# The end of one round's convolutions among the next round's: a hand-written order without a loop

## What is computed

```python
CONVS = [(128, 10, 5)] + [(128, 3, 2)] * 4 + [(128, 2, 2)] * 2     # channels, taps, stride
h = x[:, None, :]
for w, g, b, s in zip(conv_ws, ln_gs, ln_bs, strides):
    h = _conv1d(h, w, s)
    h = jnp.swapaxes(h, -2, -1)
    h = _fp32_layernorm(h, g, b)
    h = jnp.swapaxes(h, -2, -1)
    h = jax.nn.gelu(h, approximate=False)
```

## Time and profile before

| | us |
|---|---|
| median of 3 runs | 964.54 |
| lowest, highest | 959.35, 964.63 |
| the profiled execution, whole | 964.83 |
| its span, first to last instruction | 963.1 |
| TensorE busy in the span | 762.8 |
| VectorE busy | 612.2 |
| ScalarE busy | 306.3 |
| GpSimd busy | 214.3 |
| mean granted TensorE clock | 0.896 |

### The profile page before, as it was taken

How to read it: one execution, slowest core, us unless ns; L and a number is a source line. 1 busy time by engine, 2 the same in 40 slices (tenths; PEclk the granted TensorE clock), 3 DMA queues, 4 the chain that set the end, 5 groups by cost and what they waited for, 6 DMA issues and landing times. The chain is left out here.

```text
span 963.1 us, 11862 instructions
## 1 busy us (share of the span) xinstructions
PE 762.8 (79%) x4033; PEld 560.7 (58%) x4033; DVE 612.2 (64%) x1445; ACT 306.3 (32%) x505; POOL 214.3 (22%) x253
## 2 busy tenths in 40 slices
PE   0069998899989998999998625728888886489987
PEld 0026665565546664565555424617788885389977
DVE  4918555784658555244645545899888889744377
ACT  0043334333532434333312120202232331236433
POOL 3000000000000000000000030653678778318401
PEclk9999998899979898899997556859899999889999
DMA  1350420016000320000000070000000000200000
GB/s 56 43 124 1 75 65 1 0 23 118 0 2 0 68 60 0 1 1 0 1 1 1 0 303 0 1 0 1 1 0 0 0 0 0 74 1 1 1 1 25
DMA packets 22554, 25.31 MB, mean 26 GB/s; under 512 B 17052, under 2 KB 21212, under 8 KB 21404
## 3 DMA queue, kind: packets, MB, share of 16 engines
q1 hardware_dynamic: 22508, 24.74, 10.7%
HBM read 21.05 MB, written 3.66 MB: 26 GB/s over the span
## 5 line engine op out<-in xcount | busy, mean ns | idle before, releaser
L565 PE MATMUL ps<-h,w 128*128 128x400 f32 x720 | 294.8, 554 | 1.1 <-ACT h L633 0.9
L565 PEld LDWEIGHTS ps<-h,w 128*128 128x128 f32 x720 | 141.4, 203 | 106.9 <-issue 104.4
L725 DVE COPY h<-ps 128x800 f32<-128x800 f32 (+2 forms) x58 | 56.6, 975 | 97.8 <-PE ps L565 97.1
L578 PEld LDWEIGHTS ps<-averager,sq 128*100 128x100 f32 (+2 forms) x1024 | 101.9, 175 | 22.3 <-ACT sq L626 18.5
L578 PE MATMUL ps<-averager,sq 128*100 128x1 f32 (+2 forms) x1024 | 102.4, 230 | 7.8 <-ACT sq L626 7.3
L626 ACT ACTIVATE sq<-h 128x800 f32<-128x800 f32 (+2 forms) x58 | 49.9, 860 | 179.1 <-DVE h L725 179.1
L1062 PE MATMUL pt<-for_pe,ident 128*128 128x156 f32 (+2 forms) x420 | 76.9, 348 | 35.3 <-DVE for_pe L1256 35.3
L1062 PEld LDWEIGHTS pt<-for_pe,ident 128*128 128x128 f32 x420 | 69.0, 219 | 42.6 <-DVE for_pe L1256 38.7
L633 ACT ACTIVATE h<-h,lnp 128x800 f32<-128x800 f32 (+2 forms) x58 | 60.6, 1045 | 84.6 <-DVE h L756 82.8
L756 DVE TENSOR_TENSOR h<-h,ps 128x400 f32<-128x400 f32 (+2 forms) x116 | 60.0, 559 | 39.3 <-PE ps L594 39.3
L605 ACT ACTIVATE h<-ps,lnp 128x800 f32<-128x800 f32 x64 | 63.4, 1011 | 64.1 <-PE ps L526 63.9
(11 more groups left out here) (269 smaller groups left out, 1131.7 us busy)
## 6 DMA issues: line engine op xcount, KB each, us to landing
late<-windows_dram SPq DMA_DIRECT2D x24, 375.0 KB, 7.5
gate_w<-in_gate_w SPq DMA_DIRECT2D x1, 3456.0 KB, 13.0
up_w<-in_up_w SPq DMA_DIRECT2D x1, 3456.0 KB, 19.3
windows_dram<-parts SPq DMA_DIRECT2D x12, 250.0 KB, 4.9
acts<-in_down_w SPq DMA_DIRECT2D x1, 1728.0 KB, 8.2
w<-in_w SPq DMA_DIRECT2D x1, 1024.0 KB, 5.7
xs<-in_x SPq DMA_DIRECT2D x4, 252.5 KB, 4.4
out_tokens<-hidden SPq DMA_DIRECT2D x6, 96.0 KB, 1.6
```

The source lines that it names most:

```text
L565: mm = pe.matmul(out, w[:, L.first_tap + t, :], source(l, s, 2 * p + c, t), start=(t == 0), stop=(t == L.taps - 1))
L578: mm = pe.matmul(var_ps[0:L.w, at:at + 1], sq[:, n["var"] % 2, c, q * L.w:(q + 1) * L.w], averager[:, 0:1], start=True, stop=True)
L725: nc.vector.tensor_copy(joined(l, s, p, r).rearrange("p (c b) t -> p c b t", c=2), ypair[n["bank"]][:, :, 0:L.cols].rearrange("p c (b t) - ...
```

## The change

`round_plan`, walked once per round, becomes `tower_plan`, one list for all four rounds, and the loops are gone on all engines. Three things are moved in the order:

- What followed `conv(2,1,1)` in the first three rounds, that is `var` and `norm` of (2,1), its `rows` and `scale`, and all of layer three, now stands among the first four to five steps of layer one of the next round (`past` in the diff).
- Signals 0 to 8 of the next round were spread over layers two and three. They now stand all in layer two: 0 in `conv(2,1,0)`, 1 and 2 behind it, 3 in `conv(2,1,1)`, 4 behind it, then 5 to 8 in a row.
- The preparation for the round after next begins in layer two: parts 0 to 10 stand around the four steps of layer two, part 11 at the start of the next round, 12 and 13 before the fourth and fifth step of layer one. The first round's own parts 0 to 10 stand before its first step.

So that steps of two rounds can be in flight together, `rparts` and `rows` get four sets in place of two, `norm` waits for a set to be free, the variances of each layer get PSUM columns of their own, every `var` waits for the read of the `norm` before it, and `rows` waits for the copy of the `rows` before it.

```diff
+        if r == 0:
+            prep(1, 0, PREP_LATE)
+        prep(r + 1, PREP_LATE, PREP_LATE + 1)
+        conv(1, 0, 0, first(9), before(var(2, 1, 1, past), norm(2, 1, past)))
+        if past >= 0:
+            conv(3, 0, 0, first(10), var(1, 0, 0), of=past)
+            conv(1, 0, 1, before(rows(2, 1, past), var(3, 0, 0, past), scale(2, 1, 0, 1, of=past)))
+        else:
+            conv(1, 0, 1, first(10), var(1, 0, 0))
+        before(scale(2, 1, 2, 3, of=past), norm(3, 0, past))()
+        conv(1, 0, 2, first(11), var(1, 0, 1))
+        if past >= 0:
+            conv(3, 1, 0, rows(3, 0, past), var(1, 0, 2), of=past)
+        prep(r + 1, PREP_LATE + 1, PREP_LATE + 2)
+        conv(1, 0, 3, first(12), *([] if past >= 0 else [var(1, 0, 2)]), before(var(3, 1, 0, past), scale(3, 0, 0, 1, of=past), norm(3, 1, past)))
+        prep(r + 1, PREP_LATE + 2, PREP_LATE + 3)
+        conv(1, 1, 0, first(13), var(1, 0, 3), norm(1, 0))
+        before(rows(3, 1, past), scale(3, 1, 0, 1, of=past))()
+        conv(1, 1, 1, first(14), rows(1, 0), var(1, 1, 0), scale(1, 0, 0, 1))
+        scale(1, 0, 2, 3)()
+        conv(1, 1, 2, first(15), var(1, 1, 1), scale(1, 0, 4, 5))
+        scale(1, 0, 6, 7)()
+        conv(1, 1, 3, var(1, 1, 2))
+        prep(r + 2, 0, 2)
+        conv(2, 0, 0, var(1, 1, 3), norm(1, 1))
+        conv(2, 0, 1, rows(1, 1), var(2, 0, 0), scale(1, 1, 0, 1))
+        scale(1, 1, 2, 3)()
+        prep(r + 2, 2, 4)
+        conv(2, 1, 0, ahead(0), scale(1, 1, 4, 5), var(2, 0, 1), norm(2, 0))
+        ahead(1)()
+        scale(1, 1, 6, 7)()
+        prep(r + 2, 4, 6)
+        ahead(2)()
+        conv(2, 1, 1, ahead(3), rows(2, 0), var(2, 1, 0), scale(2, 0, 0, 1))
+        prep(r + 2, 6, 8)
+        ahead(4)()
+        scale(2, 0, 2, 3)()
+        prep(r + 2, 8, PREP_LATE)
+        ahead(5, 6, 7, 8)()
+        if not last:
+            return
...
-        rparts = sb("rparts", [100, 2, 4, 96], BF16)
-        rows = sb("rows", [96, 2, 400], BF16)
+        rparts = sb("rparts", [100, SETS, 4, 96], BF16)
+        rows = sb("rows", [96, SETS, 400], BF16)
...
+                    elif what == "var":
+
+                        pe.wait_ge(y_taken, number_of(plan, "conv", r, l, s, p, "pair") + 1)
+                        if n["norm"]:
+                            pe.wait_ge(var_read, n["norm"])
...
+                        if n["rows"]:
+                            pe.wait_ge(rows_ready, n["rows"])
...
+                        if n["norm"] >= SETS:
+                            dve.wait_ge(rstd_turned, n["norm"] - SETS + 1)
```

More of the change, by code:

```diff
@@ L73 @@
 TAPS = 16
+SETS = 4
+PREP_LATE = K0 + 1
 FILLERS = 10
@@ L118, in newton_rsqrt, with tower_plan @@
     steps.settle()
-def round_plan(last):
+def tower_plan():
     order = []
[L129 to L230, removed]
@@ L231, in round_plan @@
+    for r in range(ROUNDS):
+        of_round(r)
     return counted(order)
@@ L237, in counted @@
     n = dict.fromkeys(("pair", "half", "conv", "var", "norm", "rows", "scale", "gelu", "first", "prep"), 0)
-    out, bank, held = [], 0, None
-    users = [("first", -2), ("first", -1)]
-    for what, l, s, p in order:
+    n["pair"] = AHEAD
+    out, bank, held = [], AHEAD % 2, None
+    users = [("first", AHEAD - 2 + (AHEAD % 2)), ("first", AHEAD - 1 - (AHEAD % 2))]
+    for what, r, l, s, p in order:
         step = dict(n)
@@ L253, in counted, with number_of, gelus_before @@
             step["bank"], held = held, None
-        out.append((what, l, s, p, step))
+        out.append((what, r, l, s, p, step))
         n[what] += 1
         n["pair"] += what in ("conv", "first")
[L257 to L277, removed]
+    convs = [x[1:5] for x in out if x[0] == "conv"]
+    assert convs == [x[1:5] for x in out if x[0] == "var"]
+    return out
+def number_of(plan, what, r, layer, slot, p, kind):
+    return next(n[kind] for *key, n in plan if key == [what, r, layer, slot, p])
+def gelus_before(plan, r, layer, slot):
+    return {p: n["gelu"] for what, of, l, s, p, n in plan if (what, of, l, s) == ("gelu", r, layer, slot)}
 def conv_tower(nc, io, res, top):
-    body, per = round_plan(False)
-    last, _ = round_plan(True)
+    plan = tower_plan()
     sem = lambda n: top.enter_context(nc.semaphore(n))
@@ L363, in chunk @@
             if l == 3:
-                return h3[:, bass.ds(r, 1), slot, a:a + n, 0:L.pos].rearrange("p o b t -> p (o b) t")
+                return h3[:, r, slot, a:a + n, 0:L.pos]
             if l == 4:
@@ L382, in source, with batch_taken @@
             return (h4, h5)[l - 5][:, a:a + n, cut]
[L384 to L391, removed]
-                return batch + 1
[L393 to L399, removed]
+        def batch_taken(r, batch):
+            if r == 0 and batch < AHEAD:
+                return batch + 1
+            return number_of(plan, "first", r, 0, batch // GROUP, batch % GROUP, "pair") + 1
+        set_of = {(r, l, s): n["norm"] % SETS for what, r, l, s, p, n in plan if what == "norm"}
+        var_at = lambda l, k: 32 * l + k
         def joined(l, s, p, r):
@@ L409, in joined @@
             if l == 3:
-                return h3[:, bass.ds(r, 1), s, a:a + n, 0:L.pos].rearrange("p o b t -> p (o b) t")
+                return h3[:, r, s, a:a + n, 0:L.pos]
             if l == 4:
@@ L458, in _ @@
                 attention_weights(sp, io, res)
[L460 to L472, removed]
+                for r in range(1, ROUNDS):
+                    scratch = windows(r, r < ROUNDS - 1)
+                    for slot, batch in enumerate((GROUP - 1, ROUND - 1)):
+                        sp.wait_ge(y_ready, batch_taken(r - 1, batch))
+                        back(scratch, slot)
             @block.gpsimd
@@ L504, in _ @@
                                        base=-32 * a, pattern=[[-1, 8], [0, P]], channel_multiplier=1).then_inc(s_const, 1)
-                with pool.Fori(1, ROUNDS) as r:
+                for r in range(1, ROUNDS):
                     spread_phases(r)
@@ L535, in _ @@
                         pe.wait_ge(y_taken, b - 1)
[L536 removed]
+                    first(b, b % 2)
                 pe.wait_ge(weights_ready, 2)
[L539 to L550, removed]
[L551 to L595 removed]
@@ L636, in _ @@
-                for_rounds(act, run)
+                    first(b // GROUP, b % GROUP, b % 2, b)
+                for what, r, l, s, p, n in plan:
+                    L = LAYERS.get(l)
+                    if what == "first":
+                        first(s, p, n["bank"], n["pair"])
+                    elif what == "conv":
+                        act.wait_ge(y_copied, n["conv"] + 1)
+                        if n["conv"] >= 2:
+                            act.wait_ge(var_done, n["conv"] - 1)
+                        act.activation(sq[:, n["conv"] % 2, :, 0:L.cols].rearrange("p c (b t) -> p c b t", t=L.pos),
+                                       joined(l, s, p, r).rearrange("p (c b) t -> p c b t", c=2), ACT.Square).then_inc(y_taken, 1)
+                    elif what == "gelu":
+                        act.wait_ge(scaled, n["scale"])
+                        both = joined(l, s, p, r)
+                        act.activation(both, both, ACT.Gelu, scale=lnp[:, 2 * l:2 * l + 1],
+                                       bias=lnp[:, 2 * l + 1:2 * l + 2]).then_inc(gelu_done, 1)
```

262 lines of the change are left out of this document (146 added, 116 removed).

## The result

| | before | changed |
|---|---|---|
| median us | 962.63 (6 runs) | 978.24 (6 runs) |
| lowest, highest | 959.35, 966.20 | 977.12, 982.69 |
| profiled execution | 964.83 | 982.69 |
| its span | 963.1 | 981.0 |

The changed kernel takes 1.0175 times the time of the kernel before (95% interval 1.0151 to 1.0199). It is slower by 15.6 us. Its profiled execution is the slowest of its six, 4.5 us above their median, where that of the kernel before lies 2.2 us above its own; so two sets of rows laid side by side show 17.9 us (981.0 - 963.1), some 2 more than the medians. 979.8 us was forecast.

A forecast was written before the change was run, and what follows sets the result against it. TensorE was taken as the bound, losing time where it waits or runs at the lower clock. 963.1 us plus 3.0 (-39.5 + 16.8 + 15.4 + 10.3) plus 12 for clock, with 1.7 around the span, gave 979.8; range 959 to 992.

The forecast's parts named there:

- The end of a round: Behind `conv(2,1,1)`, TensorE waits for ScalarE's queue: 5.9 us lost in two rounds, 5.0 in the third, 16.8 in all.
- the sign to look for: Right behind `conv(2,1,1)`, four `first`s about 1 us apart, TensorE waiting for ScalarE, 5 to 6 us in all.
- Layer two: Waits for VectorE's late copy of `conv(2,1,0)` and for ScalarE: 6.1 us in two rounds, 3.2 in the third, 15.4 in all.
- Layer one: VectorE's queue delays `var` and `scale(3,1,0)`: 3.9 us each in rounds two and three, 2.5 in the fourth, 10.3 in all.
- Clock: Slow halves behind the new waits, three places a round: 12 us taken, between bounds of 3 and 20.
- the 39.5 removed: Time TensorE loses at the ends of three rounds in the kernel before: 12.0, 14.1 and 13.5 us, to disappear.
- The loop, counted at nothing: Taking the loop away gains 0: VectorE's 2.52 us idle behind its return costs TensorE nothing.
- The rest counted at nothing: First round's preparation hidden under the first convolution's wait, transfers hidden, added waits already met, other queues unharmed: 0 us.
- (b): Rival: a late TensorE absorbs VectorE's lateness, so the waits of layers two and one (25.7 us) vanish: 948 us, chance 0.14.
- (a): Rival: the clock stays up because the new waits are scattered; clock term 3 to 6, 971 to 974 us, chance 0.24.

The follow-up runs named there:

- e3_prep_in_gaps: The changed kernel with only layer two's preparation moved by a few steps, to where VectorE idles: 969.77 us, 1.0074 of the kernel before.
- e7_unrolled_only: The kernel before with its four loops written out and nothing else: 957.38 us, 0.9939 of the kernel before.
- e5_filled_waits: The changed kernel with matmuls of no use put into TensorE's waits in layer two and at round ends: 970.35 us, 1.0072 of the kernel before.
- e1_old_order: The changed kernel with the order of the kernel before written into its one list, nothing moved: 956.59 us, 0.993 of the kernel before.

## Why the prediction was right, point by point

- *Sign and size.* 979.8 us forecast, 978.24 measured. The direction and the places are the prediction's own; that the size came out within 2 us is in part luck. The order alone costs 21.6 us where 15.0 were forecast, and a gain of 5 to 7 us, counted at nothing, stands against it.
- *The end of a round:* three windows from signal 4 to the next `half(1,0,0)`, which hold 2.0 us of work each:

```profile
156.20:164.11 7.91, 3.57 (x13) 0.79 (x11) 7.57 (x16) 5.76 (x8) 0.00 (x0) 0.86 0.01 2
271.73:279.50 7.77, 3.40 (x13) 0.77 (x11) 7.43 (x16) 5.62 (x8) 0.00 (x0) 0.90 0.00 0
385.19:391.91 6.72, 3.23 (x14) 0.77 (x12) 1.95 (x3) 5.51 (x8) 0.00 (x0) 0.90 0.00 0
```

  7.9 us had been reckoned for the first two and 7.0 for the third: 16.3 us lost against 16.8. This step held, ScalarE's queue included. Its rows in the first round:

```profile
158.20 1.00 ACT L594 ACTIVATE h<-ps,lnp 128x800 f32<-128x800 f32 x1
160.14 1.05 ACT L616 ACTIVATE h<-h,lnp 128x800 f32<-128x800 f32 x1 [0.94 <-DVE h L738]
161.10 3.87 ACT L594 ACTIVATE h<-ps,lnp 128x800 f32<-128x800 f32 x4
```

  Counted from the end of `conv(2,1,1)` at 156.20, the gelu of signal 4 ends at 3.0, that of `scale(2,0,2..3)` at 5.0, and the four behind it follow about 1 us apart, as reckoned. Only the sign to look for was put loosely: TensorE's `first`s of signals 5 to 8 start 1.8, 2.9 and 0.9 us apart, not 1 us each.
- *Layer two.* The waits were foreseen by place and cause: 3.17 and 3.08 us for the copy, 1.29 and 0.96 for ScalarE, 1.19 and 1.29 in the third round. Counted from starts, as the prediction counts, they are 3.3 and 1.5 us against 3.5 and 1.5, and in the third round 1.4 and 1.5 against 1.6 each. From `conv(2,0,0)` to the end of `conv(2,1,1)` the three rounds take 32.96, 33.52 and 29.49 us against 24.41, 23.09 and 23.10. That is 25.4 more, less 2.0 for six moved `first`s: 23.3 us, with the lower clock in it, against 15.4 without. `e3_prep_in_gaps` shows the cause of the first part.
- *Layer one.* By cause right, by place half right: `scale(3,1,0)` waits 1.2 to 1.4 us, not 3.1, because the clock falls ahead of it (the half before it takes 3.76, 3.42 and 3.19 us) and TensorE arrives later itself. The stretch from the second half of `conv(1,0,0)` to `conv(2,0,0)`, less the moved work of 13.3 us, is 4.3, 3.1 and 5.3 us longer in rounds two to four, and the first round's, from its `half(1,0,0)`, is 2.2 longer: 14.8 against 10.3 without clock.
- *Clock.* The three halves and what follows them at a round's start cost 7.3 us more than at the higher level (the first of them 4.17 for 2.15). The rest of the clock's price sits in the two stretches above and can't be parted from the waits: they overlap, as was argued. The four terms together are 16.3 + 23.3 + 14.8 + 7.3 = 61.7 us, against 54.5 forecast. Take off the 39.5 removed: 22.2 against 15.0, where the windows of the rounds show 20.3; the 1.9 between are the error of this book-keeping. Outside the rounds the changed kernel is 2.4 us quicker, which leaves the 17.9 of the two spans. Part of the loop's gain lies in these stretches already, so the terms can't be parted cleanly from it.
- *The loop, counted at nothing:* the step that failed. Written out it gives 4.2 us by the medians of `e7_unrolled_only` (5.9 by its ratio). The argument looked at one stall on one engine and at whether TensorE waited behind it. TensorE indeed hardly waits there; it runs at the lower clock level for longer (0.86 against 0.97 in the stretch above). About this much the terms of the order were low, and so the sum came out right.
- *The rest counted at nothing* held: the first round starts at 64.6 us against 64.1, and no wait of TensorE inside the rounds is for a transfer.
- *The rivals.* (b), that a late TensorE absorbs VectorE's lateness, is true for some 2 us at each `scale(3,1,0)`; the other waits are there nearly as reckoned. (a), that the clock stays up, is refuted by the halves of 3.87 to 4.37 us behind the waits, which are 2.3 us long at the higher level, and by `e5_filled_waits`: if it stayed up, nothing would be gained by keeping it up.
- *What the prediction didn't see* is what lies beneath each wait. It priced the row of first-layer steps at 16.8 us plus clock. Taking the row away gave 16.8 us in all, since VectorE's queue came to light behind it, 6.3 us in one round and 6.2 in the next. And the preparation alone costs 27 us in the old order; nothing in the prediction puts near so much down to it.

## What to carry to other kernels

Filling one engine's idle time by work from the next round pays only if the order of the other two engines' queues is rebalanced with it: against `e1_old_order`, nearly the same interleaving was worth +22 us and -32 us, by where VectorE's preparation and the steps that need ScalarE stand. Cut side work to the length of the gap behind each copy, and put none of it ahead of an instruction that frees a buffer for the engine that is the bound. When a wait is removed, look at what the next queue has ready at that moment: that is the new time, not zero.

## What the runs showed of the hardware that was not expected

- A loop over two rounds, written out, made the program 0.6% faster (0.9939, interval 0.9915 to 0.9963), though its return showed only one idle stretch, 2.52 us on VectorE, which TensorE did not wait for. The Trainium skill, "Runtime: NRT & Kernel Launch", section "Instruction fetch mechanics", says that a taken branch whose target lies outside the pages already fetched stalls the engine until the target has come. The row at the loop's return agrees with such a stall; that it was one, no run here shows. On TensorE the gain is time at the higher clock level (0.97 for 0.86 over some 40 us), and why is open.
- Behind waits of 0.2 to 2.4 us in a row of short matmuls stood a half at the lower level (4.37 us, 3 of 3 round ends), and matmuls that compute nothing, put into these waits and those of layer two, took 7.9 us off the program, though three of the six halves behind them stayed at 3.8 us or more.
